# One product with ones per group, a third addition on VectorE, and projections begun ahead of the products for maxima

## The reference

```python
shift, scale, gate = split(silu(cond) @ mod_w + mod_b, 3)
h = layernorm(x) * (scale + 1.0) + shift
q, k, v = split(h @ w_qkv)              # 16 heads of 32 each
q, k = rope(layernorm(q, q_norm_w)), rope(layernorm(k, k_norm_w))
attn = softmax(q @ k.T / sqrt(32))      # over the keys
out = x + (attn @ v) @ w_out * gate
```

## Time and profile before

| what | value |
|---|---|
| median of 3 runs | 1742.82 us (1742.61 to 1743.07) |
| profiled execution | 1738.36 us, span 1736.6 us |
| busy: TensorE, VectorE | 1669.5 us (96%), 1247.1 us (72%) |
| busy: ScalarE, GpSimd | 1034.1 us (60%), 680.7 us (39%) |
| products with ones (line 475) | 2016 instructions, 161.9 us busy |
| mean granted clock of TensorE | 0.988 of full speed |

### The profile page before, as it was taken

How to read it: one execution, slowest core, us unless ns; L and a number is a source line. 1 busy time by engine, 2 the same in 40 slices (tenths; PEclk the granted TensorE clock), 3 DMA queues, 4 the chain that set the end, 5 groups by cost and what they waited for, 6 DMA issues and landing times.

```text
span 1736.6 us, 34608 instructions
## 1 busy us (share of the span) xinstructions
PE 1669.5 (96%) x13350; PEld 1007.4 (58%) x13350; DVE 1247.1 (72%) x1667; ACT 1034.1 (60%) x1610; POOL 680.7 (39%) x707
## 2 busy tenths in 40 slices
PE   5978899999999999999999999999999999999887
PEld 3734556665666666666566666666656666665444
DVE  8767677777777777777777777777777777776553
ACT  3445666666666666566666666666666666665552
POOL 0523243344344344334434434433443443443322
PEclk9979999999999999999999999999999999999999
DMA  6034355554645555555555555555555546454553
GB/s 214 25 68 85 82 129 113 134 116 110 137 113 125 125 122 119 119 127 117 122 125 126 112 130 117 119 131 116 122 116 126 131 107 143 104 113 107 128 122 110
DMA packets 55432, 204.48 MB, mean 118 GB/s; under 512 B 6872, under 2 KB 6872, under 8 KB 39144
## 3 DMA queue, kind: packets, MB, share of 16 engines
q0 software_dynamic: 18144, 132.13, 39.1%
q1 hardware_dynamic: 37128, 70.14, 12.0%
HBM read 53.25 MB, written 16.88 MB: 40 GB/s over the span
## 4 chain that ended last, share of the span: by engine, by line
PE 92%; DVE 5%; issue 1%; DMA 1%; POOL 1%; ACT 0%; SPq 0%; ACTq 0%; DVEq 0%; POOLq 0%
PE O L459 13%; PE SA L440 13%; PE Y L345 12%; PE Y L358 10%; PE Y L348 9%; PE Y L352 9%; PE Y L475 8%; PE SM L397 6%; PE MB L380 3%; PE SA L444 3%; PE SA L335 1%; PE SA L418 1%; DVE cst L1074 1%; DVE cst L1066 1%; PE MB L408 1%
## 5 line engine op out<-in xcount | busy, mean ns | idle before, releaser
L819 ACT ACTIVATE probs<-SM 128x1024 f32<-128x1024 f32 x256 | 262.3, 1025 | 235.1 <-PE SM L444 226.3
L1066 DVE TENSOR_REDUCE cst<-SM 128x2 fp32r<-128x1024 f32 x236 | 289.1, 1225 | 153.4 <-PE MB L397 153.4
L1315 POOL DMA_DIRECT2D probs<-probs x126 | 109.8, 871 | 594.0 <-ACT probs L821 541.1
L1066 DVE TENSOR_REDUCE cst<-MB 128x2 fp32r<-128x1024 f32 x236 | 287.0, 1216 | 0.0
L459 PE MATMUL O<-probs,vals 128*32 128x512 f32 x2048 | 270.9, 601 | 0.0
L1296 POOL TENSOR_TENSOR pair_part<-rows,rope_pair 128x256 f32<-128x256 f32 x128 | 119.6, 935 | 382.8 <-DVE rows L1043 381.9
L821 ACT ACTIVATE probs<-SA 128x1024 f32<-128x1024 f32 x256 | 262.4, 1025 | 0.0
L345 PE MATMUL Y<-wqkv_hi,hT_hi 128*128 128x512 f32 x716 | 215.4, 423 | 0.0
L715 ACT ACTIVATE rows<-Y 128x512 f32<-128x512 f32 x121 | 72.4, 599 | 205.0 <-PE Y L352 205.0
L348 PE MATMUL Y<-wqkv_hi,hT_lo 128*128 128x512 f32 x716 | 193.9, 392 | 0.5 <-DVE hT_lo L1049 0.5
L1055 DVE SCALAR_TENSOR_TENSOR qk_lo<-MB,pass_w,qk_hi 128x512 fp32r<-128x512 f32 x128 | 90.3, 746 | 144.8 <-ACT qk_hi L751 144.7
(11 more groups left out here) (221 smaller groups left out, 3557.0 us busy)
## 6 DMA issues: line engine op xcount, KB each, us to landing
probs<-probs POOLq DMA_DIRECT2D x126, 1024.0 KB, 7.7
xin<-in_x_dram SPq DMA_DIRECT2D x62, 256.0 KB, 7.4
xres<-in_x_dram SPq DMA_DIRECT2D x60, 256.0 KB, 2.6
out_dram<-xres SPq DMA_DIRECT2D x60, 256.0 KB, 5.7
shift_scale<-mod_rows SPq DMA_DIRECT2D x15, 512.0 KB, 3.7
gate<-mod_rows SPq DMA_DIRECT2D x16, 256.0 KB, 5.4
rows<-in_L_cond_mod_w_dram SPq DMA_DIRECT2D x2, 1024.0 KB, 9.0
probs<-in_L_cond_w_qkv_dram SPq DMA_DIRECT2D x2, 1024.0 KB, 13.3
```

The source lines that it names most:

```text
L819: act.activation(probs[:, a, 2:4, :], SM[:], ACT.Exp).then_inc(s_exp, 1)
L1066: dve.tensor_reduce(heads[:, 2 * half:2 * half + 2, 0], bank[:], AX.X, ALU.max, negate=True).then_inc(max_out, 1)
```

## The change

Per group there is one product with ones, of 512 columns, behind key block 2 of the next slot. The sum that was made in steps behind it is made on the probabilities: after the two DMAs VectorE adds block 0's buffer to block 2's (`sum_keys`, 128 x 2048 elements), ahead of the maxima of product 1. For groups 59 and up VectorE adds nothing, and TensorE multiplies both buffers with ones into one sum. ScalarE's copies and VectorE's two additions of sums go, and `log_sums` reads `Y`, between the two exponentials of block 2. The probabilities change their buffers in another ring (`homes`), with a fifth buffer in `rows` for the last four groups, and so wait for other readers.

On TensorE `begin_projection` issues two products of V's projection ahead of product 0 and one of K's ahead of product 3; two products of the output projection move ahead of product 1. In the first five slots x is transposed into `Y` instead of `SA[:, 1]`: key block 2 doesn't wait for `hT_lo` there, and the product with ones does. In the last slot two residual tiles lie in `shift_scale`, and two output products move as in the other slots.

```diff
-    def probs_buffer(g, t):
-        return t ^ (g % 2)
+    homes, spare = [(0, 1, 2, 3)], TT
+    for g in range(1, NS):
+        b = homes[-1]
+        if g < NS - NG:
+            homes.append((b[1], b[3], b[0], b[2]))
+        else:
+            homes.append((spare, b[1], b[3], b[0]))
+            spare = b[2]
...
+        def key_probs(g, t):
+            if homes[g][t] == TT:
+                return rows[:, 0, 0:2].rearrange("p t j n -> p (t j) n")
+            return probs[:, homes[g][t]]
...
-                if n - 6 >= 0:
-                    pe.wait_ge(s_exp, 2 * (TT * (n - 6) + 1) + 2)
+                if FT <= n < FT + 5:
+                    pe.wait_ge(v_out, n - 1)
+                elif n >= FT:
+                    pe.wait_ge(s_exp, 2 * (TT * (n - FT) + 1) + 2)
                 for k in range(DT):
-                    mm = pe.transpose(SA[:, 1, k * P:(k + 1) * P], x_rows(n)[:, k * P:(k + 1) * P], ident[:])
+                    mm = pe.transpose(x_bank(n)[:, k * P:(k + 1) * P], x_rows(n)[:, k * P:(k + 1) * P], ident[:])
...
+            def begin_projection(n, j, bank, count):
+                x_hi, _ = x_buffers(n)
+                cols = slice(j * D, (j + 1) * D)
+                pe.wait_ge(h_hi, n + 1)
+                for k in range(count):
+                    pe.matmul(bank, x_hi[:, k, :], wqkv_hi[:, k, cols], start=(k == 0), stop=False)
+            def project(n, j, bank, begun=0):
                 x_hi, x_lo = x_buffers(n)
...
-                for k in range(DT):
+                for k in range(begun, DT):
                     pe.matmul(bank, x_hi[:, k, :], wqkv_hi[:, k, cols], start=(k == 0), stop=False)
...
-                if t == 2 and tile(g + 6):
+                if t == 2 and g >= 5 and tile(g + 6):
...
-            def add_over_keys(g, t, h):
-                pe.wait_ge(first_added if t == 0 else second_added, 16 * (g + 1))
-                if h == 1 or t == 2:
-                    pe.wait_ge(first_summed, 2 * g + (1 if t == 0 else 2))
-                if h == 1 and t == 2:
-                    pe.wait_ge(sum_added, 2 * g + 1)
-                if t == 0 and h == 0 and g > 0:
-                    pe.wait_ge(sum_added, 2 * g)
-                cols = half_cols(h)
-                for i in range(HG):
-                    mm = pe.matmul(Y[head_rows(i), cols], ones_r[:, 0:E].bitcast(F32),
-                                   probs[:, probs_buffer(g, t), i, cols],
-                                   start=True, stop=True, skip_group_check=True)
+            def add_over_keys(g):
+                if late(g):
+                    pe.wait_ge(first_added, 16 * (g + 1))
+                    pe.wait_ge(second_added, 16 * (g + 1))
+                else:
+                    pe.wait_ge(keys_summed, g + 1)
+                parts = (0, 2) if late(g) else (2,)
+                for t in parts:
+                    for i in range(HG):
+                        mm = pe.matmul(Y[head_rows(i), :], ones_r[:, 0:E].bitcast(F32),
+                                       key_probs(g, t)[:, i, :],
+                                       start=(t == parts[0]), stop=(t == 2), skip_group_check=True)
                 mm.then_inc(ones_done, 1)
...
                 scores_by_key(s, 0)
                 if s > 0:
+                    weigh_values(s - 1, 3)
+                if s > 0 and tile(s + 4):
+                    if s > 1:
+                        pe.wait_ge(sum_ln, s - 1)
                     if tile(s + 5):
                         pe.wait_ge(raw_out, raw_count(s + 5, 1))
-                    if s == LAST:
-                        pe.wait_ge(y_gated, NT - TT - 1)
-                    add_over_keys(s - 1, 0, 1)
-                    weigh_values(s - 1, 3)
+                    begin_projection(s + 4, 2, Y[:], 2)
                 if late(s + 1):
                     scores_by_query_half(s + 1, 0, 0)
                 elif group(s + 1):
                     scores_by_query(s + 1, 0)
                 if s > 0 and tile(s + 4):
-                    pe.wait_ge(first_summed, 2 * s)
-                    project(s + 4, 2, Y[:])
+                    project(s + 4, 2, Y[:], 2)
...
                 scores_by_key(s, 1)
                 if late(s + 1):
                     scores_by_query_half(s + 1, 1, 0)
-                if s > 0:
-                    if tile(s + 4):
-                        pe.wait_ge(v_out, s + 5)
-                    add_over_keys(s - 1, 2, 0)
                 weigh_values(s, 0)
                 if s == LAST:
                     add_last_sums(0)
+                n = s - 5 if s < LAST else NT - TT - 1
+                if n >= 0:
+                    pe.wait_ge(o_high, n + 1)
+                    pe.wait_ge(sum_ln, s - 1)
+                    if tile(s + 4):
+                        pe.wait_ge(v_out, s + 5)
+                    if n == 0:
+                        pe.wait_ge(wout_low, 1)
+                    if s == LAST:
+                        pe.wait_ge(y_gated, NT - TT - 1)
+                    project_out(n, Y[:], 0, 2)
                 if late(s + 1):
                     scores_by_query_half(s + 1, 1, 1)
                 elif group(s + 1):
                     scores_by_query(s + 1, 1)
-                n = s - 5 if s < LAST else NT - TT - 1
                 if n >= 0:
-                    if n == 0:
-                        pe.wait_ge(wout_low, 1)
                     pe.wait_ge(o_low, n + 1)
-                    pe.wait_ge(sum_added, 2 * s - 1)
-                    project_out(n, Y[:], 0, 4)
+                    project_out(n, Y[:], 2, 4)
                 if tile(s + 6):
...
                 if s > 0:
                     if n >= 0:
                         pe.wait_ge(y_gated, n + 1)
-                    add_over_keys(s - 1, 2, 1)
+                    else:
+                        pe.wait_ge(h_hi, s + 7)
+                        pe.wait_ge(h_lo, s + 7)
+                    add_over_keys(s - 1)
                 weigh_values(s, 1)
...
                 if tile(s + 6):
                     if s > 0:
-                        pe.wait_ge(sum_added, 2 * s)
+                        pe.wait_ge(sum_ln, s)
                     else:
-                        pe.wait_ge(v_out, s + 5)
+                        pe.wait_ge(h_lo, s + 7)
                     project(s + 6, 0, Y[:])
...
                 scores_by_key(s, 3)
                 if late(s + 1):
                     scores_by_query_half(s + 1, 3, 0)
-                if group(s + 1):
-                    if tile(s + 6):
-                        pe.wait_ge(raw_out, raw_count(s + 6, 0))
-                    add_over_keys(s, 0, 0)
                 weigh_values(s, 2)
                 if s == LAST:
                     add_last_sums(2)
-                    pe.wait_ge(sum_added, 2 * LAST)
+                    pe.wait_ge(sum_ln, LAST)
                     project_last(1, 0, 2)
+                if tile(s + 6):
+                    pe.wait_ge(raw_out, raw_count(s + 6, 0))
+                    begin_projection(s + 6, 1, Y[:], 1)
...
                 if tile(s + 6):
-                    pe.wait_ge(first_summed, 2 * s + 1)
-                    project(s + 6, 1, Y[:])
+                    project(s + 6, 1, Y[:], 1)
...
-            def move_first_sum(g, h):
-                act.wait_ge(ones_done, 4 * g + h + 1)
+            def log_sums(g, sums):
+                act.wait_ge(ones_done, g + 1)
                 if g > 0:
                     act.wait_ge(o_scaled, g)
                 else:
                     act.wait_ge(parts_out, 3)
-                cols = half_cols(h)
...
+                    elif g > 0 and t == 0:
+                        act.wait_ge(pv_step, TT * (g - 1) + 2)
+                        act.wait_ge(first_added, 16 * g)
+                    elif g > 0 and t == 1:
+                        act.wait_ge(pv_step, TT * g)
+                        act.wait_ge(second_added, 16 * g)
+                    elif g > 0 and t == 2:
+                        act.wait_ge(keys_summed, g)
+                    elif g > 0:
+                        act.wait_ge(ones_done, g)
...
-                if s > 0:
-                    move_first_sum(s - 1, 1)
                 key_exponentials(s, 0, 1)
                 if s > 0:
...
                 key_exponentials(s, 2, 0)
+                if s > 0:
+                    log_sums(s - 1, Y[:])
                 key_exponentials(s, 2, 1)
                 if s > 0:
-                    log_sums(s - 1, sum_inv[:])
                     inverse_sums(s - 1)
                 if s == LAST - 1:
                     output_high(s - 4)
...
-                if s < LAST:
-                    move_first_sum(s, 0)
                 key_exponentials(s, 3, 1)
                 if 0 <= s - 4 and s < LAST - 1:
...
                                   ).then_inc(max_out, 1)
-            def add_sums(g, h):
-                dve.wait_ge(ones_done, 4 * g + 3 + h)
-                dve.wait_ge(first_summed, 2 * g + 1 + h)
-                cols = half_cols(h)
```

(24 more changed lines are left out.)

63 lines of the change are left out of this document (22 added, 41 removed).

## The result

The changed kernel is slower: 1749.91 us (median of 14 runs, 1744.09 to 1750.47) against 1742.94 us (median of 14, 1737.99 to 1747.04), a ratio of 1.0033 with a 95% interval of 1.0022 to 1.0045. That is a third of a percent, +3.8 to +7.8 us; the two medians are 7.0 us apart. Its profiled execution took 1749.95 us, span 1748.2 us, and so stands at its median. That of the kernel before was one of its shorter ones, so the two profiles differ by 11.6 us, more than the medians do.

The account below looks back on a forecast made before the run. TensorE was taken as the bound (92% of the chain). First slots -10.4, middle +1 and last slots +4.9 gave -4.5 us, hence 1738 us from the median, range 1726 to 1751.

Parts of the forecast that it names:

- Comes off TensorE: Middle slots: four 256-column products with ones go, one of 512 comes; 0.86 us less TensorE work a slot.
- Early starts on TensorE: Products of V, K and output projections begun early add 0.44 us a slot, leaving TensorE 25.15 us of work.
- the bound of 0.6: Upper bound on the early starts' cost per slot, if each of three shape switches pays a full 0.2 us.
- The path through `hT_lo`: Middle slots: 16.04 us to product 0 plus 9.55 through VectorE to key block 2, 25.59 us with 0.44 wait.
- "The order alone": Middle slots: even with an addition of no length, the path from product 0 through product 1 gives 25.43 us.
- What the early starts buy: Ahead of maxima's products: one or two early products cover the exponentials' wait, so the maxima's product doesn't stand.
- First five slots: Slots 0 to 4: shorter waits 3.7 us, three clock losses gone 4.6, slot 0 2.1; sum -10.4 us.
- The rival of the falling clock: First slots: the clock falls anyway, so 4.6 us less is gained: 1743 us, no change; chance 0.11.
- Last slots: Slots 58 to 63: +0.9, +1.4, +0.6 for each of 60 to 62, +0.8; sum 4.9 us, bounds 2 and 9.
- the slower rival: VectorE's sum comes later or takes longer: +13 us, 1751; slower than before from 0.15 us a slot; chance 0.18.
- an overlap: GpSimd still running when VectorE's sum begins: up to 2.2 times as long, +1 us a slot, 1791; chance 0.03.

Follow-up runs that it names:

- experiment 6: Changed kernel with one V and one output product begun early instead of two, and VectorE's statistics of x at the slot's start: 1729.35 us against 1743.61, ratio 0.9915.
- experiments 3: Changed kernel with VectorE's addition cut to one column of 2048 and a bias added to the logarithm's input: 1733.37 us.
- experiment 4: Changed kernel with VectorE's statistics of x moved from behind product 0's maxima to the start of the slot: 1739.20 us.
- second pair of profiles: Both kernels run once more, unaltered: the changed kernel took 1749.06 us, the kernel before 1739.69 us.
- experiment 2: Changed kernel with no product begun early, the output projection whole behind product 1: 1741.56 us, ratio 0.9987.
- experiment 1: Kernel before with only x of tiles 6 to 10 transposed into Y in the first five slots: 1732.24 us against 1743.42, ratio 0.9936.

## Why the prediction was wrong, step by step

- **Comes off TensorE:** right, 0.87 us for 0.86, the new product at 0.88 for 0.89. But the base was 25.54 a slot, not the 25.57 of one slot.
- **Early starts on TensorE:** 0.66 instead of 0.44, above the bound of 0.6, so TensorE's own work is 25.33 us a slot and not 25.15. More than half of the miss is the price of the single product begun for K. It was taken as 0.31, a row's price for the last product ahead of another shape, with its other end among its like; here both ends meet another shape, and it holds 0.44. The price for two (0.65) was right at 0.66. The rest lies in the output projection, which grew by 0.25 and not 0.18 (mean of slots 10 to 49, experiment 6).
- **The path through `hT_lo`:** right in mechanism. The sum said 25.59 with a wait of 0.44; measured are 25.70 and a wait of 0.36. The first part was 0.13 longer than forecast (16.17 in the mean of slots 10 to 49), which is the 0.13 of K's product: this is the step that failed in the middle slots. The VectorE part was right within 0.02. A difference of 0.16 instead of 0.02 a slot makes 7.6 of the 16.1 us by which the profile misses the forecast's sum.
- **"The order alone":** forecast 25.43, measured 25.565 in experiments 3 and 4. This path has the same first part and misses by the same 0.13, and it alone would have left the middle of the kernel without a gain.
- **What the early starts buy:** named but not weighed. Cover was taken as worth having because a wait would appear without it. On TensorE alone it is: without the starts the waits cost 0.9 us a slot, with them 0.66 is put on (25.51 us a slot against the 25.33 of experiment 6). But V's starts lie in full on both paths to `hT_lo`, and with two products begun the path takes more than the cover gives: 25.70 against 25.51 with no start at all. That one product covers the wait as well as two was not considered.
- **First five slots:** -8.8 instead of -10.4 (-9.1 in the second pair of profiles). The waits went as forecast, and slot 3 takes 24.51 for 24.46, but the clock still falls in slots 1 and 4 (3 and 4 in the second profile). The rival of the falling clock was half true. That the sum came so near is luck: slot 0 got 4.0 us shorter instead of 2.1, at a clock of 0.84 against 0.72, and so made up for a part of the two falls.
- **Last slots:** this step failed by as much as the middle, 7.4 us (12.3 for 4.9). The prediction added only waits to the lengths of before, and so put a falling clock at nothing without a reason. At a clock of 1.00 its sizes hold: slot 60 +0.6 (forecast +0.6), slot 58 +0.8 (forecast +0.9). The rest can be priced at like order: slot 61 against slot 60 is 23.19 - 21.68 = 1.5; slot 59, by the kernel before at 0.93 and at 1.00 (24.18 - 22.69), 1.5; slot 62 against the same slot in experiment 2, where it kept 1.00 and took 23.38 (though without the early output products), 4.2. That is 7.2 of the 12.3 us, and it leaves 5.1 for all waits, where 4.9 was forecast. The 5.1 also hold what the lower clock of the last slot costs (0.92 against 0.96), which has no like slot to price it by, so the agreement is no finer than a microsecond or so.
- **Rivals:** VectorE's sum was not late because of a DMA or GpSimd (no idle time in front of it, 2281 ns), so of the slower rival only its result came true: from 0.15 us a slot on it is slower, and 0.16 it was. The mechanism was the forecast's own. GpSimd computes nothing while the sum runs (`o_lo` ends at 814.17, the sum starts at 821.27), so what an overlap would do to it was not met.

What stays open is the rule by which the clock falls. TensorE stood ahead of the falls whose traces were read, but the length of one stand doesn't decide it: the same stand of 1.65 us ahead of slot 59 was followed by a full clock in one execution of the kernel before and by a fall in the other. The stand of 1.76 or 1.77 us in slot 58 was followed by a full clock in both profiles of the changed kernel and by a fall in experiment 4. In experiment 1 slots 60, 61 and 62 have the same three stands (1.32, 1.32 and 0.40 us), and only slot 60 has a fall. Nor was it tried what the changed kernel would take with no fall at all: the 7.2 us are a sum of differences between like slots, not a run.

## What to carry to other kernels

Where an early start fills a wait, weigh the wait against all that the start costs: two changes of shape on its engine, and its whole length on any loop that passes through that place. Begin one instruction, not two, if one covers the wait. A saving on the engine that is full is worth only what the next loop leaves: work out the length of every loop that closes within a period, and shorten those first. Experiment 6 did so and took the middle slots from 25.70 to 25.33 us, 0.2 below the kernel before. And price a change from the distances of starts: busy time grows a little at every wait. In stretches where TensorE already stands, price a longer stand with the clock that it may cost.

## What the runs showed of the hardware

- In slot 58 stands of TensorE of 2.00 to 2.52 us came with a fall of the clock in all four traces that have them, stands of 1.76 and 1.77 us in one of three. From 1.76 to 2.52 us the slot grew from 25.16 to 28.20, four times what was added to the stand.
- The falls can be as regular as the schedule (slots 59, 61 and 62 in two profiles, equal within 0.02 us) or differ from run to run (slots 3, 4 and 59 of the kernel before, slots 1 and 3 of the changed one).
- One product on the whole array (128*128) between the values (128*32) and the product for the maxima (32*128) holds 0.44 us, two hold 0.66, and one in a long row 0.23. Whether one or two are begun early leaves TensorE's total work the same (1343.56 and 1343.00 us in 53 slots).
- VectorE's addition of 2048 fp32 columns from SBUF takes 2281 ns beside the work of TensorE and ScalarE and the DMAs, as in the kernel's first 40 us. GpSimd computes nothing at that time.
